# ScalarE function tables loaded by the kernel's own calls, one set for sines and output gates, and a token's gates from a tangent

## The reference

```python
def ffn(x):                                     # x: 2048 rows; 8 experts, the best 2 of each row
    logits = x @ gate_w
    top_logits, top_idx = top_k(logits, 2)
    top_gates = softmax(top_logits)             # two numbers a row that add up to 1
    gates = sum(one_hot(top_idx) * top_gates)
    h = gelu(x @ w1[e] + b1[e])                 # for the chosen experts
    routed = gates * (h @ w2[e] + b2[e])
    return routed + gelu(x @ shared_w1 + shared_b1) @ shared_w2 + shared_b2

def attn(x):
    z = causal_conv4(x @ W_mem); k_val, s_raw = split(z)      # 32 heads x 8, and 32 scores
    q = x @ W_q
    p_w = exp(clip(scale * s_raw, -20, 20) + log_w)           # log_w from position and slopes
    re_k, im_k = cos(k_val * theta), sin(k_val * theta)       # 8 angles for each value
    state = cumsum(p_w * [re_k, im_k]) / cumsum(p_w)
    out_re, out_im = sums over the 8 angles of state * q
    y_val, y_gate = split(out_re @ W_re + out_im @ W_im)
    return (y_val * silu(y_gate)) @ W_out

x = x + 0.5 * ffn(layernorm(x))
x = x + attn(layernorm(x))
x = x + 0.5 * ffn(layernorm(x))
```

## Time and profile before

| what | us |
|---|---|
| median of 3 runs | 1300.2 |
| lowest and highest run | 1297.55 and 1307.3 |
| the profiled execution, as timed | 1298.54 |
| its span in the profile | 1297.3 |
| busy in it: PE / DVE / ACT / POOL | 1018.4 / 718.9 / 586.2 / 447.5 |

### The profile page before, as it was taken

One profiled execution on the slowest core, in us unless ns is written; L12 is line 12 of the kernel. 1 busy time (PEld: TensorE's weight loads), 2 busy tenths in 40 slices (PEclk: granted clock), 3 DMA queues, 4 the chain that ended last, 5 costly groups with the idle time before them and its releaser, 6 DMA issues.

```text
span 1297.3 us, 10733 instructions
## 1 busy us (share of the span) xinstructions
PE 1018.4 (78%) x3296; PEld 562.8 (43%) x3296; DVE 718.9 (55%) x1162; ACT 586.2 (45%) x1003; POOL 447.5 (34%) x428
## 2 busy tenths in 40 slices
PE   6999779972969869969946379877976897979884
PEld 3547545422525435445412144344443543546552
DVE  4311000077779979979998978889977810200000
ACT  4324333323415768567423254268475741214332
POOL 4164443202453343332000227144354212244442
PEclk9999998995878979988987779889988999789888
DMA  8955554424154656675333742367775525035554
GB/s 299 373 155 97 99 89 74 78 61 137 27 105 109 165 118 138 134 211 148 83 99 77 198 113 51 81 177 147 147 209 121 80 36 108 30 73 96 94 92 53
DMA packets 60204, 155.15 MB, mean 120 GB/s; under 512 B 10578, under 2 KB 10578, under 8 KB 57974
## 3 DMA queue, kind: packets, MB, share of 16 engines
q0 software_dynamic: 29568, 60.90, 27.7%
q1 hardware_dynamic: 30582, 93.58, 23.9%
HBM read 99.74 MB, written 58.88 MB: 122 GB/s over the span
## 4 chain that ended last, share of the span: by engine, by line
DMA 37%; PE 25%; DVE 15%; POOL 8%; ACT 7%; issue 7%; SPq 1%; POOLq 0%; ACTq 0%; DVEq 0%
DMA out_rows<-ys,into_i 14%; DMA x_rows<-ys,into_i 12%; PE hps L736 5%; POOL slots L1526 4%; PE misc L867 4%; DMA xs<-x_normal,rows_i 3%; PE yps L748 3%; DVE run L1343 3%; DMA xin<-x_rows 2%; PE yps L805 2%; PE xps L719 2%; ACT ys L975 2%; PE hps L789 2%; PE misc L833 2%; DVE trig L1350 1%
## 5 line engine op out<-in xcount | busy, mean ns | idle before, releaser
L805 PE MATMUL yps<-w_all,hidden_sb 128*128 x368 | 194.5, 656 | 47.8 <-ACT hidden_sb L962 47.2
L789 PE MATMUL hps<-w_all,hidden_sb 128*128 x736 | 182.4, 393 | 4.0 <-ACT hidden_sb L945 4.0
L789 PEld LDWEIGHTS hps<-w_all,hidden_sb 128*128 128x128 f32 x736 | 143.0, 200 | 47.8 <-issue 31.2
L1343 DVE TENSOR_TENSOR_SCAN run<-pwx,trig 128x512 f32<-128x512 f32 x128 | 149.4, 1208 | 24.0 <-ACT trig L1046 23.4
L1538 POOL DMA_INDIRECT xs<-x_normal,rows_i x92 | 106.9, 1162 | 109.3 <-PE xps L780 82.1
L1551 POOL DMA_INDIRECT x_rows<-ys,into_i x46 | 82.7, 1797 | 158.3 <-DMA x_rows<-ys,into_i 84.9
L736 PE MATMUL hps<-xnT,sw_sb 128*128 128x512 f32 x256 | 130.8, 666 | 7.5 <-ACT hidden_sb L935 6.8
L975 ACT ACTIVATE ys<-yps,slots 128x512 f32<-128x512 f32 x92 | 62.9, 685 | 160.5 <-DMA out_rows<-ys,into_i 61.6
L1551 POOL DMA_INDIRECT out_rows<-ys,into_i x46 | 81.0, 1761 | 152.3 <-DMA out_rows<-ys,into_i 76.3
L805 PEld LDWEIGHTS yps<-w_all,hidden_sb 128*128 128x128 f32 x368 | 70.4, 203 | 117.5 <-issue 115.6
L748 PE MATMUL yps<-sw_sb,hidden_sb 128*128 128x512 f32 x256 | 118.4, 605 | 0.0
(11 more groups left out here) (193 smaller groups left out, 1570.8 us busy)
## 6 DMA issues: line engine op xcount, KB each, us to landing
qx<-q_cols SPq DMA_DIRECT2D x128, 256.0 KB
x_normal<-xin SPq DMA_DIRECT2D x32, 256.0 KB, 3.2
w_all<-in_w_experts SPq DMA_DIRECT2D x8, 1024.0 KB, 9.0
xin<-x_rows SPq DMA_DIRECT2D x32, 256.0 KB, 6.6
turns_sb<-in_w_out SPq DMA_DIRECT2D x3, 1536.0 KB, 10.4
xin<-in_x SPq DMA_DIRECT2D x16, 256.0 KB, 3.6
x_rows<-ys POOLq DMA_DIRECT2D x16, 256.0 KB, 4.6
q_cols<-xin SPq DMA_DIRECT2D x16, 256.0 KB
```

Source lines behind the costliest of these rows:

```text
L789: t = PE.matmul(hps[:, bank, 0:H], xT[:, j % 2, c, :], w_all[:, bass.ds(expert[j] + c * H, H)], start=c == 0, stop=c == KC - 1)
L805: t = PE.matmul(yps[:, bank, :], hb[:, j % 2, ec, :], w_all[:, bass.ds(expert[j] + (KC * H + ec * D), D)], start=ec == 0, stop=ec == EC - 1)
L1343: t = VE.tensor_tensor_scan(run[:, c, :], pwx[:, n // M, :], trig[:, n % 2, c, :], 0.0, ALU.mult, ALU.add)
```

## The change

Three things change, and with them the planner's input.

- ACT's sets are loaded by calls of a new function `functions(name)`, which does nothing when that set is the one loaded last. The call is the first thing that a stage puts into ACT's queue, ahead of all its waits. `waves()` and `output_gate()` ask for the same set.
- The gates of a row are made from tanh(difference / 2), written over `diff`. `gate_weights()` loads a set only where none is loaded yet; in the built program no load stands ahead of any tangent, whether the set of Gelu, of Exp or of Silu is loaded there. The two gates are 0.5 - 0.5 t and 0.5 + 0.5 t, two DVE instructions that don't wait for each other.
- The planner's `gates` on ACT has no table any more, and `gates` on DVE costs 1.9 and not 2.2. Nothing else of its costs changes, but with these numbers it makes another order for all five engines.

```diff
-            piece("ACT", ("gates", q), 0.3, ("DVE", ("rank", q)), *([("DVE", ("gates", q - 1))] if q else []), table="exp")
-            piece("DVE", ("gates", q), 2.2, ("ACT", ("gates", q)), *([("PE", ("gT", q - 1))] if q else []),
+            piece("ACT", ("gates", q), 0.3, ("DVE", ("rank", q)), *([("DVE", ("gates", q - 1))] if q else []))
+            piece("DVE", ("gates", q), 1.9, ("ACT", ("gates", q)), *([("PE", ("gT", q - 1))] if q else []),
...
+            loaded = [None]
+            def functions(name):
+                if loaded[0] != name:
+                    SE.preload_act_table_set(name)
+                    loaded[0] = name
...
             def gate_weights(q):
                 act.wait_ge(*ranking.at((q, 2)))
-                if q > 0:
-                    act.wait_ge(*gating.at((q - 1, 3)))
-                SE.activation(gr[:, :, 1], diff[:, :], ACT.Exp).then_inc(*gate_exp.of(q))
+                if loaded[0] is None:
+                    functions("gelu_and_others")
+                SE.activation(diff[:, :], diff[:, :], ACT.Tanh, scale=0.5).then_inc(*gate_exp.of(q))
 
             def gelu(q, n):
+                functions("gelu_and_others")
                 act.wait_ge(*hidden_made.at((q, n)))
...
             def block_gelu(g, j):
+                functions("gelu_and_others")
...
             def weights(b):
+                functions("exp_and_others")
                 act.wait_ge(*p_log.at((b, 3)))
...
             def waves(b, n):
+                functions("silu_and_others")
...
             def output_gate(b, v):
+                functions("silu_and_others")
...
                 if q > 0:
-                    vec.wait_ge(*gate_exp.at(q - 1))
+                    vec.wait_ge(*gating.at((q - 1, 2)))
...
                 vec.wait_ge(*gate_exp.at(q))
-                VE.tensor_scalar(diff[:, :], gr[:, :, 1], 1.0, None, ALU.add).then_inc(*gating.of((q, 0)))
-                vec.wait_ge(*gating.at((q, 0)))
-                VE.reciprocal(gr[:, :, 0], diff[:, :]).then_inc(*gating.of((q, 1)))
-                vec.wait_ge(*gating.at((q, 1)))
-                VE.tensor_tensor(gr[:, :, 1], gr[:, :, 1], gr[:, :, 0], ALU.mult).then_inc(*gating.of((q, 2)))
+                VE.tensor_scalar(gr[:, :, 0], diff[:, :], -0.5, 0.5, ALU.mult, ALU.add)
+                VE.tensor_scalar(gr[:, :, 1], diff[:, :], 0.5, 0.5, ALU.mult, ALU.add).then_inc(*gating.of((q, 2)))
```

More of the change, by code:

```diff
@@ L587, in macaron @@
         ranking = signal("s_ranking", [(q, i) for q in staged("rank", "DVE") for i in range(5)])
-        gating = signal("s_gating", [(q, i) for q in staged("gates", "DVE") for i in (0, 1, 2, 7, 3, 4, 5, 6)])
+        gating = signal("s_gating", [(q, i) for q in staged("gates", "DVE") for i in (2, 7, 3, 4, 5, 6)])
         placing = signal("s_placing", [(g, i) for g in range(NG) for i in (*range(8), 19, *range(8, 19))])
```

## The result

| kernel | median us | runs | profiled execution (span) |
|---|---|---|---|
| before | 1303.63 | 1297.55 to 1307.3 (4) | 1298.54 (1297.3) |
| changed | 1325.4 | 1321.56 to 1329.97 (4) | 1322.25 (1321.0) |

The ratio is 1.0185, with a 95% interval of 1.0147 to 1.0222: slower by 22 us in the medians and by 23.7 us in the profiled executions, where I had forecast 6 us less and a range of 1277 to 1307. The 1300.2 that stands ahead of the prediction is the median of the first three of these four runs of the kernel before.

A forecast was written before the change was run, and what follows sets the result against it. From 340 to 1030 us DVE was taken as the bound, elsewhere chains of indirect adds or PE. Terms summed to -5.0 us, 1293.5 from the profiled 1298.54 or 1295.2 from the median; forecast 1294, range 1277 to 1307.

The forecast's parts named there:

- (d): Weights of batch 1: their Exp moves directly behind a block copy, DVE's 3.40 us wait goes, 1.1 us won.
- (f): Second output gate of batch 0: the Gelu moves ahead of the late block, one load leaves the path, 1.3 us won.
- (g): Job 4: logits and gates come later, so DVE gets a new wait; 3.2 us lost, between 0 and 5.
- more switches: Rival: 97 loads against 90 in the former order, seven switches cost 9.0 us among blocks; 1307.5, chance 0.17.
- all loads leave the path: Rival: every load on the chain that ended last falls into idle time, 20.5 us gone; 1277, chance 0.20.
- (a): Job 1's gates: no Exp, so no Gelu load at 69.88; PE and group 0's adds come 1.28 us earlier.
- (b): First sine of batch 0: its load moves inside ACT's wait for the phase, a query copy starts sooner; 1.0 us won.
- (c): Gates on DVE: three dependent instructions become two independent ones, 0.3 us each; 0.9 us for jobs 3, 4 and 5.
- (e): Sines whose phase came late: three loads on the chain move into ACT's waits; two of them win 2.6 us.

The follow-up runs named there:

- e2: Kernel before with only the planner's two numbers changed, so the new order with the code of before (115 loads): 1319.06 us, ratio 1.0168.
- e5: Changed kernel and its order, with Silu in place of Gelu in jobs and blocks (12 loads left): 1314.57 us, ratio 1.0147.
- e6: Changed kernel's code in the order of before, with Silu in place of Gelu in jobs and blocks (12 loads left): 1298.35 us, ratio 0.9983.
- e1: Changed kernel with the planner's two numbers of before, so every engine's order is the former one (90 loads): 1299.97 us, ratio 1.001.
- e4: Changed kernel with the gates still marked in the planner as a switch to the Exp's set; a fourth order, 95 loads: 1315.06 us, ratio 1.0182.
- e9: Changed kernel's code in the order of before, except the blocks of group 0 in the new order: 1302.99 us, ratio 1.0005.
- e11: Changed kernel's code in the order of before, with one pair on POOL exchanged (group 2's fourth add ahead of its tenth block's gather): 1303.72 us, ratio 1.0015.
- e12: Changed kernel with POOL alone in its former order, every other engine in the new one: 1325.77 us, ratio 1.0187.
- e13: Changed kernel and its order, but each sine up to two pieces of block work sooner in ACT's queue (91 loads): 1327.07 us, ratio 1.0182.

## Why the prediction was wrong

**The step that failed** is how the new order was priced: as the sum of the places that I had looked at ((d), (f) and (g)), with the rest put at nothing without a reason, and in the rival by the seven more loads alone. The runs show in its place 16 to 22 us that are the order's own: e2 lost 1.68% without any edit of the code, and e5 against e6 lost 16 us with the loads gone as well. The rival "more switches" had the sign and a chance of 0.17, with its far end beyond 1313, but not the mechanism: its 9.0 for seven loads isn't there. The sign that I had named for it, a sum of DVE's waits for ACT that grows, came (39.1 to 54.8 us for sines and output gates), but it was no sign of loads: with 12 loads left these waits still grow, from 29 us in e6 to 41 in e5.

Its counterpart is the second miss: "all loads leave the path" was bounded by 20.5, the loads on the chain. e6 took 78 of 90 away and won nothing that can be measured. I take it that a load on the chain ends last there only by little, with the block's rows or the phase behind it as late; no run shows this place by place. The sum of (a), (b), (c) and the whole loads of (e), 5.8 us or 0.45%, lies outside e1's interval, which ends at 0.29% faster.

The terms, by the changed kernel's trace:

- (a) The load at 70 is gone, and PE waits there for 0.40 us instead of 1.68. "Next late is PE itself" was wrong: PE then waited 0.76 us for the gathered block, and the first add of group 0 came at 112.79, not at 107.9. The difference can't be put down to the change: in the other kernels the scaled sum ahead of that add starts anywhere from 106.3 (e4, load gone) to 114.8 (e2, load still there). The clock, below, makes 2.8 of the 3.7 us between the two executions.
- (b) Right: load inside the wait, sine 0.03 us behind the absolute value, and the copy at 285.89, 3.64 us behind the start of PE's query matmuls (282.25) instead of 4.67: 1.03 won, as I had it. Behind it the chain now has a fetch of rows of 15.00 us, where it had the store of the queries of 14.08; job 3's statistics began 19.82 us behind those matmuls instead of 19.97, so 0.15 of the 1.03 was left there.
- (c) Right: 0.23 us instead of 0.57 for job 3's gates.
- (d) Right in kind: the reciprocal runs without a wait and DVE waits 0.75 us for the convolution instead, which began 19.9 us behind the list of group 1 and 22.6 before: 2.7 won, not 1.1.
- (e) Loads stand ahead of the absolute values as foreseen; no gain of these can be seen in e1.
- (f) As foreseen a sine, not a Silu, stands behind the late block. I had counted one load saved there; what counted is that DVE now waits 9.61 us for that sine and 1.18 for the gate behind it, where it waited 6.92 and 1.73 for two gates: +2.1 instead of -1.3.
- (g) Neither wait came: DVE was late itself, having waited 6.87 us for batch 2's rows at 613.91, and ranked at 633.25 without a wait. The place cost, but by the blocks' adds: the chain there runs from the last add of group 1 (606.90) to the fetch of those rows (612.29).

Pairs of bring and add on POOL cost nothing, as said (e9, e11, e12). What of the order costs it is settled only so far: not the loads, not the tangent, not group 0, not POOL's queue, not the place of the sines on ACT as far as e13 moved them, not two products on DVE. What is left is how the queues of PE, ACT and DVE stand to each other in groups 1 and 2; that is argued from what fell, and the mechanism stays open. One place shows what it looks like: four scans in a row of group 2's stretch waited for sines in the changed kernel, 9.0 us together, and the same four in the kernel before, from 856.6 to 884.7 us, waited for none (one product between them waited 3.6 us for its queries):

```profile
874.66 2.34 DVE L1355 TENSOR_TENSOR_SCAN run<-pwx,trig 128x512 f32<-128x512 f32 x2 [3.56 <-ACT trig L1059]
884.58 2.41 DVE L1355 TENSOR_TENSOR_SCAN run<-pwx,trig 128x512 f32<-128x512 f32 x2 [1.74 <-ACT trig L1059]
895.00 2.34 DVE L1355 TENSOR_TENSOR_SCAN run<-pwx,trig 128x512 f32<-128x512 f32 x2 [2.16 <-ACT trig L1059]
904.87 2.34 DVE L1355 TENSOR_TENSOR_SCAN run<-pwx,trig 128x512 f32<-128x512 f32 x2 [1.57 <-ACT trig L1059]
```

Which queue carries it can't be found by exchanging whole parts: by the planner's own list of what follows what, PE's or ACT's part of group 1 or 2 stands in a circle of waits unless PE's, ACT's and DVE's are all exchanged. No kernel tried is faster than the one before.

The Trainium skill, "ScalarE: Activation LUTs", section "Table sets: the hidden batching unit", which I had cited for the rival, says to batch activations by set, all of one set and then all of the other. Here 78 switches fewer gave 0.9983 (0.9941 to 1.0025) in the former order, and orders with 84 to 88 loads were slower than one with 106: the measurement decides, and in this kernel the count is no guide.

## What to carry to other kernels

A number in a planner is an edit of every queue. Price it by two kernels, the new code in the old order and the old code in the new order, before reasoning about any one instruction. Loads, or anything else, that lie on the chain that ended last are a bound, not a gain, as long as nothing shows how late the work behind them is; and in this interleaving a move of sines by up to two places in one queue cost 1.3 to 1.4% either way, so a rewritten order has to be measured. Here no rewritten order was faster.

## What the runs showed of the hardware

**Clock.** In the head PE's granted clock fell to its lower level, 1.2 GHz, for a few us between 97 and 112 us. It did so in the profiled execution of every kernel here but the one before, of which there is one profile. The window of the changed kernel, PEclk third from the end:

```profile
101.00:107.00 6.00, 6.00 (x21) 5.17 (x22) 1.51 (x15) 0.37 (x1) 0.00 (x0) 0.50 0.18 52
```

The same window of the kernel before:

```profile
101.00:107.00 6.00, 5.97 (x32) 4.81 (x32) 1.66 (x16) 3.64 (x8) 1.94 (x2) 1.00 0.44 116
```

Ahead of it, in both, stand 32 matmuls of 128x8, the logits of job 2; in the changed kernel PE had also stood idle for 0.76 us. The eight matmuls of a block behind them took 3.76 us at the lower level and 1.97 at the higher. It came in e2, which has the code of before, with no idle time ahead as well, and in e1, which has the order of before. So the 2.8 us that it makes between the two profiled executions are neither the code's nor the order's alone; whether the kernel before always goes without it, one execution can't say.

**POOL and DVE.** That DVE's order alone stretched a POOL piece from about 3 to 7.5 us I hadn't expected. The Trainium skill, "SBUF — State Buffer", section "Who interferes with whom", says that the two share a port pair, and that a DVE instruction with two inputs in SBUF contends with a GpSimd instruction that reads SBUF. The rows agree: the long piece ran beside products, sums and a scan, and ended 0.8 us behind the start of the first one-input instruction that followed them. That the port is what it waited for no run here shows by itself.
